# Macaron MoE layer on one core: the second expert stage scatters into the output, and GpSimd's accumulating transfers add the residuals

## What is computed

```python
def ffn(x):                      # x: layer-normed tokens, N = 4096, C = 128, H = 256, E = 8
    idx = argmax(x @ router.T)   # one expert for each token
    y = down[idx] @ (silu(gate[idx] @ x) * (up[idx] @ x))
    ys = (silu(x @ w_gate_s.T) * (x @ w_up_s.T)) @ w_down_s.T     # shared expert, all tokens
    return y + ys

x = x + 0.5 * ffn(layernorm(x))
x = x + attn(layernorm(x))       # circular convolution, decaying causal sum, correlation
x = x + 0.5 * ffn(layernorm(x))
```

## Time and profile before

| what | value |
|---|---|
| median of 3 runs | 293.18 us (292.18 to 294.78) |
| profiled execution, its own time | 292.21 us |
| its span in the trace | 290.5 us |
| PE busy | 257.8 us (89%) |
| DVE busy | 189.4 us (65%) |
| POOL busy | 179.4 us (62%) |
| ACT busy | 160.3 us (55%) |
| DMA: MB moved, mean | 27.51 MB, 95 GB/s |

### The profile page before, as it was taken

How to read it: one execution, slowest core, us unless ns; L and a number is a source line. 1 busy time by engine, 2 the same in 40 slices (tenths; PEclk the granted TensorE clock), 3 DMA queues, 4 the chain that set the end, 5 groups by cost and what they waited for, 6 DMA issues and landing times.

```text
span 290.5 us, 6435 instructions
## 1 busy us (share of the span) xinstructions
PE 257.8 (89%) x1788; PEld 215.9 (74%) x1788; DVE 189.4 (65%) x734; ACT 160.3 (55%) x374; POOL 179.4 (62%) x260
## 2 busy tenths in 40 slices
PE   0889999979999999986699999999779999999980
PEld 0547677558999999845577878676469999999560
DVE  4796664954555555448999999676845556655355
ACT  2744353236777777326498877732157777777210
POOL 6646777713777777723457888767505758887700
PEclk9999999999999999997679999899999999999997
DMA  6871111323333321144000101101423433311078
GB/s 210 314 310 40 55 47 60 109 69 80 101 98 107 98 78 38 38 122 172 0 1 23 35 28 38 49 29 56 124 66 88 107 88 105 92 55 48 27 250 329
DMA packets 24244, 27.51 MB, mean 95 GB/s; under 512 B 4967, under 2 KB 17645, under 8 KB 23952
## 3 DMA queue, kind: packets, MB, share of 16 engines
q1 hardware_dynamic: 17648, 16.06, 18.6%
q0 software_dynamic: 4544, 8.54, 9.0%
q10 hardware_dynamic: 2016, 2.50, 2.4%
HBM read 15.37 MB, written 12.62 MB: 96 GB/s over the span
## 4 chain that ended last, share of the span: by engine, by line
PE 45%; POOL 17%; DVE 14%; issue 12%; DMA 4%; ACT 3%; SPq 1%; DVEq 1%; ACTq 0%; POOLq 0%
PE bank L960 13%; PE bank L883 12%; POOL returned L386 10%; PE bank L891 6%; PE bank L968 6%; POOL dispatched L357 3%; DMA xres<-in_x 3%; PE bank L908 3%; PE bank L914 2%; DVE st_f L558 2%; DVE hs L631 2%; DVE xres L599 2%; POOL token L380 1%; PE bank L869 1%; POOL scale_f L346 1%
## 5 line engine op out<-in xcount | busy, mean ns | idle before, releaser
L386 POOL DMA_INDIRECT returned<-ey,token x78 | 76.6, 982 | 32.9 <-issue 18.0
L960 PE MATMUL bank<-xsT,wgu 128*128 128x128 f32 x624 | 82.9, 276 | 2.5 <-DVE xres L599 1.5
L960 PEld LDWEIGHTS bank<-xsT,wgu 128*128 128x128 f32 x624 | 75.7, 192 | 3.7 <-DVE xres L599 1.8
L357 POOL DMA_INDIRECT dispatched<-xn,slot x64 | 63.5, 993 | 23.7 <-issue 17.7
L883 PE MATMUL bank<-xnT,gu 128*128 128x512 f32 x128 | 65.1, 636 | 4.3 <-DVE hs L631 3.5
L813 DVE COPY ey<-bank 128x128 f32<-128x128 f32 x78 | 22.8, 292 | 45.6 <-PE bank L968 45.5
L489 ACT ACTIVATE wgu<-gu 128x512 f32 x78 | 48.2, 623 | 4.1 <-issue 3.9
L462 ACT ACTIVATE sg<-bank 128x512 f32<-128x512 f32 x32 | 18.9, 591 | 54.5 <-PE bank L883 47.1
L968 PE MATMUL bank<-wdn,eh 128*128 128x128 f32 x312 | 47.5, 276 | 0.5 <-DVE eh L808 0.5
L511 ACT ACTIVATE eg<-bank 128x256 f32<-128x256 f32 x78 | 29.9, 384 | 32.6 <-PE bank L960 32.4
L968 PEld LDWEIGHTS bank<-wdn,eh 128*128 128x128 f32 x312 | 40.9, 192 | 0.9 <-DVE eh L808 0.9
(11 more groups left out here) (102 smaller groups left out, 292.9 us busy)
## 6 DMA issues: line engine op xcount, KB each, us to landing
xs<-dispatched SPq DMA_DIRECT2D x80, 66.0 KB, 1.8
ey<-returned SPq DMA_DIRECT2D x16, 256.0 KB, 4.3
gu<-in_gu SPq DMA_DIRECT2D x1, 2048.0 KB, 12.6
out<-xres ACTq DMA_DIRECT2D x8, 256.0 KB, 2.9
returned<-ey,token POOLq DMA_INDIRECT x78
xres<-in_x SPq DMA_DIRECT2D x1, 1024.0 KB, 8.1
dn<-in_dn SPq DMA_DIRECT2D x1, 1024.0 KB, 15.1
dispatched<-xn,slot POOLq DMA_INDIRECT x64
```

Of the source, the lines that this page charges most:

```text
L357: nc.gpsimd.indirect_dma_start(dispatched[:, :], bass.IndirectOffsetOnAxis(slot[:, i:i + 1], 0), xn[:, i, :], None, bounds_check=last_row) ...
L386: nc.gpsimd.indirect_dma_start(returned[:, :], bass.IndirectOffsetOnAxis(token[:, b:b + 1], 0), ey[:, b, :], None, bounds_check=last_back, ...
L960: last = nc.tensor.matmul(bank[4 + b % WR][:, i * P:(i + 1) * P], wgu[:, b % WR, i * P:(i + 1) * P], xsT[:, b // 2 % 2, b % 2, :], start=T ...
```

## The change

In the second FFN only:

- `send` scatters into the output itself (`home[1]`) instead of `returned`.
- `evac_y` multiplies by 0.5 on its way from PSUM (a tensor_scalar in place of a copy), so the scattered rows are half of y.
- SyncE's eight reads of `returned` and VectorE's eight sums go, and with them ScalarE's eight stores. VectorE's last shared part is no longer placed among the sums.
- GpSimd, at the end of its program, waits for all scatters to have landed, and then for each group for `half_done`, and issues one transfer from `xres` to the output with `accum_op=ALU.add`: the transfer adds the 256 KB of the group to what stands in the output. Line numbers of the new kernel are a few higher than before.

```diff
+    home = [returned[:, :], out.rearrange("b t c -> (b t) c")]
...
-                sp.wait_ge(blk_out, 16 * NB * (f + 1))
-                for k in range(G):
-                    sp.dma_start(groups(back, k, k + 1), returned_dram[:, k:k + 1, :]).then_inc(back_in[k], 16)
+                if f == 0:
+                    sp.wait_ge(blk_out, 16 * NB)
+                    for k in range(G):
+                        sp.dma_start(groups(back, k, k + 1), returned_dram[:, k:k + 1, :]).then_inc(back_in[k], 16)
             sp.wait_ge(stored, 16 * G)
...
                     nc.gpsimd.indirect_dma_start(
-                        returned[:, :], bass.IndirectOffsetOnAxis(token[:, b:b + 1], 0),
+                        home[f], bass.IndirectOffsetOnAxis(token[:, b:b + 1], 0),
                         ey[:, b, :], None, bounds_check=last_back, oob_is_err=False).then_inc(blk_out, 16)
...
             experts(1)
+            pool.wait_ge(blk_out, 16 * NB * 2)
+            for k in range(G):
+                pool.wait_ge(half_done, G + k + 1)
+                nc.gpsimd.dma_start(out_dram[:, k:k + 1, :], groups(xres, k, k + 1),
+                                    accum_op=ALU.add).then_inc(stored, 16)
...
-            for k in range(G):
-                act.wait_ge(x3_done, k + 1)
-                act.dma_start(out_dram[:, k:k + 1, :], groups(xres, k, k + 1)).then_inc(stored, 16)
...
                 def evac_y(b):
                     dve.wait_ge(blk_dn, f * NB + b + 1)
-                    nc.vector.tensor_copy(ey[:, b, :], y_of(b)).then_inc(blk_y, 1)
+                    if f == 0:
+                        nc.vector.tensor_copy(ey[:, b, :], y_of(b)).then_inc(blk_y, 1)
+                    else:
+                        nc.vector.tensor_scalar(ey[:, b, :], y_of(b), 0.5, None, ALU.mult).then_inc(blk_y, 1)
...
-            for g, part in SHARED_PARTS[LATE:-1]:
+            for g, part in SHARED_PARTS[LATE:]:
                 shared(1, g, part)
-            for k in range(G):
-                add_back(1, k, x3_done)
-                if k == 2:
-                    shared(1, *SHARED_PARTS[-1])
```

More of the change, by code:

```diff
@@ L207, in build @@
         blk_dn, blk_y = sem("blk_dn"), sem("blk_y")
-        x3_done, stored = sem("x3_done"), sem("stored")
+        stored = sem("stored")
         block = ctx.enter_context(nc.Block())
@@ L600, in add_half, with add_back @@
                                                op0=ALU.mult, op1=ALU.add).then_inc(done, 1)
[L602 to L605, removed]
+            def add_back(k):
+                dve.wait_ge(back_in[k], 16)
+                dve.wait_ge(half_done, k + 1)
+                add_half(k, tiles(back, k), x1_done)
             def scan(k):
@@ L723, in add_first @@
                 if valid(k + 4):
-                    add_back(0, k + 4, x1_done)
+                    add_back(k + 4)
                     dve.wait_ge(x1_done, k + 5)
```

## The result

The changed kernel takes 295.16 us, the kernel before 293.21 us in the same runs (medians of 16 each). The ratio is 1.0072, 95% interval 1.0045 to 1.0099: 2.1 us slower (1.3 to 2.9). The ratio compares the usual executions alone, without the few slow ones (297.36 before, 299.35 after); over all 16 the medians are 1.95 us apart. The forecast was 0.4 us faster.

The account below looks back on a forecast made before the run. Full DMA engines were taken to bound the tail: bytes from 278.2, 10.6 us to 288.8, plus 1.27 us of end gives 290.1 against 290.5, -0.4 us, so 292.8 us; range 289.4 to 299.0.

Parts of the forecast that it names:

- What bounds the tail: Tail after the last scatter: 11.6 us of full DMA engines moving 4.19 MB, with VectorE's eight sums beside it.
- The doubled read: Tail: adding transfers read output rows as well as `xres`, 4.19 MB at 394 GB/s, 10.6 us.
- so from 278.2: Tail: first bytes at 278.2, from the issue at 276.65, SyncE's 1.04 us and 0.55 us for GpSimd's longer issue.
- and with the 1.27 us of the end: Kernel end: 1.27 us from last bytes to span's end, kept from before, taking 288.8 to 290.1.
- a span outside 289.3 to 291: Whole kernel: the prediction's sign of being wrong, if the profiled span leaves 289.3 to 291 us.
- the issue: Tail: GpSimd issues every 1.28 us, the eighth at 285.6, landing at 288.2 or 289.2.
- Cheap transfers: Tail rival: second read hidden, issue every 1.06 us or faster, group 7 decides; gain 2.8 to 3.8 us; chance 0.17.
- Dearer issue: Tail rival: GpSimd's adding transfers 2.26 us from start to start; 5.5 us slower, 298.7; chance 0.18.
- Slow adding: Tail rival: engines read 4.19 MB at 273 GB/s, 15.4 us; 4.4 us slower, 297.6; chance 0.20.
- Evacuation with 0.5: Second expert stage: 0 to 51 ns more for each of 39 blocks, at most 2.0 us; taken as 0.
- The rule of the Trainium skill: Tail: two source reads share one ring, ratio 1.93; by its engine rate 248 GB/s, 8.5 us, end at 288.0.

Follow-up runs that it names:

- scalar_stores: Changed kernel with its eight transfers only storing `xres`, nothing added, issued by ScalarE instead of GpSimd: 288.71 us, ratio 0.9881.
- half_half: Changed kernel with only groups 0 to 3 added by GpSimd's transfers; groups 4 to 7 read back, summed and stored by ScalarE: 294.16 us, ratio 1.0022.
- plain_store: Changed kernel with GpSimd's eight transfers only storing `xres`, nothing added: 291.56 us, ratio 0.9953.
- gpsimd_stores: Kernel before with the tail's eight plain stores issued by GpSimd instead of ScalarE: 295.41 us, ratio 1.0073.

## Why the prediction was wrong

- **What bounds the tail** (full DMA engines, not the chain's VectorE): right. With the sums gone, the engines were full for as long as before (11.55 us) and nothing was gained; with plain stores alone, which halve the bytes, 3.5 us were gained (scalar_stores).
- **The doubled read**: right in size. The adding doubled the engines' time for a byte (178 ns against 85 for 2 KB); that a second read does it is not shown. The bytes took 11.55 us against 10.6: at 202 GB/s of result 2.10 MB would take 10.4 us, but the first two microseconds ran at 106 and 137 GB/s, which costs 0.8 us, and the next three at 182, which costs 0.3.
- **"so from 278.2"**, the start: right in sum. From the issue to the first bytes it was 1.26 us and not 1.55 (whose added 0.55 is 0.52 by its own numbers, 0.98 less 0.46), and the wake-up took 0.29 us more than SyncE's, of which I had counted 0.04.
- **"and with the 1.27 us of the end"**: this is the step that failed. I carried the end of the kernel before over as a constant of the program. It belongs to an end at which only ScalarE's and SyncE's queues have work. GpSimd's drain lasts 2.0 us past its last landing, and the end measured 2.95 us: 1.68 more than the term. With 0.95 more for the bytes, and the wake-up (+0.25) and the way to the first bytes (-0.29) that cancel, this makes 2.6 us, from -0.4 to +2.16. The trace of before had the drain in it, hidden (278.73 against a landing at 276.59), and I read there only what the program's end waited for, not which engine would come last to the meeting once GpSimd had the last transfers. The same end is missing where the prediction goes by the issue: 288.2, 289.2 and the cheap case's 286.7 to 287.7 are landings, compared with a span's end of 290.5 as if nothing stood between them. It was 0.41 us before and is 2.21 now. No case of the prediction had it, and by its own sign (a span outside 289.3 to 291) it was wrong: 293.5.
- **Cheap transfers**: half right. The issue is cheap: 0.54 to 0.64 us from start to start, where I had taken 1.28. The price of the adding is not hidden.
- **Dearer issue**: wrong for direct transfers, right in kind for the adding scatter, which the change doesn't use (1.55 us, 1.85 and more from start to start).
- **Slow adding**: its limit was 11.03 us for the bytes, and 11.55 were measured, so it held by half a microsecond, at 363 GB/s of read side instead of 273. It alone would have made the change 0.5 us slower, by this sum.
- **Evacuation with 0.5**: 0, as taken. The 39 tensor_scalars take as long as the 39 copies:

```profile
L818 DVE COPY ey<-bank 128x128 f32<-128x128 f32 x39 | 11.4, 291 | 23.4 <-PE bank L971 23.4
L820 DVE TENSOR_SCALAR ey<-bank 128x128 f32<-128x128 f32 x39 | 11.4, 292 | 22.2 <-PE bank L971 22.2
```

The rule of the Trainium skill that spoke against the change ("Collectives: The Full Stack", section "The bandwidth ceiling: the fold count and why AG ≠ RS ≠ AR": two source reads halve the rate) agrees with this trace: 202 GB/s added against 373 stored by the same queue, a ratio of 1.85, where the page has 1.93. The page's case is a reduction between cores, and no row here shows the reads. Its rate for one engine, from which the prediction estimated 248 GB/s, came out too high: 202 GB/s were measured.

## What to carry to other kernels

In this kernel, the transfers that add saved instructions and semaphores, not DMA time: count their bytes twice, and ask what bounded the stretch before. Whoever moves the last transfers of a kernel to another engine's queue moves the end too, since all engines meet there and GpSimd came 1.7 to 2.2 us after its last landing. Read the meeting of the engines at the end of the trace before and after, and have other engines' transfers land some 2 us after GpSimd's last one. Only half_half bears on this last advice: ScalarE's last store landed 1.4 us after GpSimd's last transfer, the wait at the end was 0.4 us, and the time was lost elsewhere.

## What the runs showed of the hardware that I had not expected

- GpSimd's closing drain ended 1.97 to 2.16 us after its last landing in four kernels (before, after, plain_store, gpsimd_stores); with one store alone on its queue in the tail it was 1.69 us, in both traces.
- A direct transfer of 128 rows of 2 KB takes GpSimd 0.54 us to issue, an indirect one of 128 rows of 512 bytes 0.98, and an adding indirect one 1.55.
- GpSimd's plain stores left in packets of 4 KB, the adding ones in packets of 2 KB. GpSimd's queue after shows 5696 packets; with the adding left out it is 512 fewer, and their share of the span is 10.9% instead of 13.2%:

```profile
q0 software_dynamic: 5184, 10.63, 10.9%
```

- A read back beside adding transfers landed up to 9.09 us after its issue (half_half); beside GpSimd's plain stores it was at most 5.9 (gpsimd_stores).
